# Masks of the local scores written on 64x32 tiles of TensorE in a DiT block with causal and local attention

## What is computed

```python
bk2, bv2 = (look(bk), look(bv))          # each window of 32 tokens sees itself and the window before
mask = (it < jb) | (it > jb + w) | (jb == -1)
sim = jnp.einsum('bhwie,bhwje->bhwij', bq, bk2) * QK_SCALE
sim = jnp.where(mask, -jnp.finfo(sim.dtype).max, sim)
attn = jax.nn.softmax(sim, -1)
```

## Time and profile before

| | us |
|---|---|
| median of 3 runs | 3508.06 |
| lowest, highest | 3505.7, 3515.55 |
| span of the profiled execution (first to last instruction) | 3495.1 |
| PE busy in the span | 3309.7 (95%) |
| POOL, DVE, ACT busy | 2907.1, 2951.4, 2468.4 |

### The profile page before, as it was taken

How to read it: one execution, slowest core, us unless ns; L and a number is a source line. 1 busy time by engine, 2 the same in 40 slices (tenths; PEclk the granted TensorE clock), 3 DMA queues, 4 the chain that set the end, 5 groups by cost and what they waited for, 6 DMA issues and landing times.

```text
span 3495.1 us, 158019 instructions
## 1 busy us (share of the span) xinstructions
PE 3309.7 (95%) x69988; PEld 1936.2 (55%) x69988; DVE 2951.4 (84%) x3104; ACT 2468.4 (71%) x3349; POOL 2907.1 (83%) x2483
## 2 busy tenths in 40 slices
PE   7999999779999999999999999999999999999997
PEld 4666666445555555555555555555555555555553
DVE  6888888688888988888888889888998889988873
ACT  5777777556777767777677777676877777767764
POOL 3665555588999989999899999898999999989993
PEclk9999999999999999999999999999999999999997
DMA  1000000154645545545455454555554554545452
GB/s 67 5 5 5 5 5 5 44 119 102 143 114 130 120 115 126 131 112 127 113 126 127 106 137 110 129 120 121 120 135 105 142 124 109 140 108 134 102 124 62
DMA packets 163861, 347.33 MB, mean 99 GB/s; under 512 B 32876, under 2 KB 42352, under 8 KB 153840
## 3 DMA queue, kind: packets, MB, share of 16 engines
q1 hardware_dynamic: 163184, 337.23, 40.9%
HBM read 24.62 MB, written 4.19 MB: 8 GB/s over the span
## 4 chain that ended last, share of the span: by engine, by line
PE 70%; DVE 11%; POOL 6%; issue 6%; ACT 4%; SPq 2%; DMA 1%; DVEq 0%; POOLq 0%; ACTq 0%
PE psA L697 29%; PE psB L697 23%; PE psB L559 8%; PE psA L559 6%; PE psB L754 3%; DVE h L1338 3%; DVE pt L1237 1%; SPq L490 1%; PE psA L754 1%; DVE negm L1342 1%; DVE sum L1349 1%; DVE ts L1330 1%; DVE h L1320 1%; DMA kf<-h 1%; POOL sq L1443 1%
## 5 line engine op out<-in xcount | busy, mean ns | idle before, releaser
L1410 POOL TENSOR_TENSOR pt<-wk,pt 128x256 f16<-128x256 f32 (+3 forms) x256 | 368.1, 1455 | 288.7 <-ACT pt L939 199.0
L1443 POOL TENSOR_TENSOR sq<-sq 128x512 f32<-128x512 f32 x384 | 488.5, 1281 | 79.6 <-ACT sq L1022 78.2
L1438 POOL TENSOR_TENSOR h<-h,ts 128x512 f32<-128x512 f32 x384 | 499.8, 1302 | 1.2 <-DVE ts L1330 1.2
L1439 POOL TENSOR_TENSOR h<-h,ts 128x512 f32<-128x512 f32 x384 | 497.1, 1295 | 0.0
L1338 DVE TENSOR_TENSOR h<-h,psB 128x1024 f32<-128x1024 f32 x288 | 337.8, 1215 | 57.1 <-PE psB L697 55.5
L1463 POOL TENSOR_TENSOR pb<-pb,rc 128x1024 f32<-128x1024 f32 x192 | 366.3, 1908 | 8.8 <-DVE rc L1351 8.8
L1320 DVE TENSOR_TENSOR h<-psA,t_rot 128x1024 f32<-128x1024 f32 x192 | 234.2, 1220 | 72.7 <-ACT sq L1022 65.7
L697 PE MATMUL psA<-kf,qf 64*32 64x64 f32 x18432 | 251.2, 224 | 22.0 <-issue 21.6
L697 PEld LDWEIGHTS psA<-kf,qf 64*32 64x32 f32 x18432 | 191.5, 106 | 124.8 <-issue 124.4
L1320 DVE TENSOR_TENSOR h<-psB,t_rot 128x1024 f32<-128x1024 f32 x192 | 233.4, 1216 | 26.2 <-ACT sq L1022 20.4
L1022 ACT ACTIVATE sq<-psA 128x1024 f32<-128x1024 f32 x192 | 197.0, 1027 | 63.7 <-PE psA L697 63.5
(11 more groups left out here) (368 smaller groups left out, 10242.0 us busy)
## 6 DMA issues: line engine op xcount, KB each, us to landing
qf<-h SPq DMA_DIRECT2D x768, 136.0 KB
kf<-h SPq DMA_DIRECT2D x768, 136.0 KB, 2.5
vev<-vo SPq DMA_DIRECT2D x288, 256.0 KB
vev<-vo SPq DMA_DIRECT2D x96, 192.0 KB
stage<-wqk SPq DMA_DIRECT2D x24, 256.0 KB, 5.0
stage<-wvl SPq DMA_DIRECT2D x12, 256.0 KB, 4.1
stage<-wof SPq DMA_DIRECT2D x12, 256.0 KB, 5.5
xb<-xt SPq DMA_DIRECT2D x8, 256.0 KB, 7.9
```

What stands on the lines that cost most here:

```text
L1410: e.tensor_tensor(pt[g][pr][:, :, 1, o:o + w], wk[(slot_of(s)[0] - 1) % SLOTS][:, :, 0:w], pt[g][pr][:, :, 0, o:o + w], ALU.subtract).then ...
L1438: e.tensor_tensor(halves_of(h, 0), halves_of(h, 0), t[1], ALU.subtract)
L1439: e.tensor_tensor(halves_of(h, 1), halves_of(h, 1), t[0], ALU.add).then_inc(ended["ad"])
L1443: e.tensor_tensor(sqb[c][:, 0, :], sqb[c][:, 0, :], sqb[c][:, 1, :], ALU.add).then_inc(ended["qa"])
```

## The change

The masks of a score tile are written by 16 products in place of four. Each takes 32 of the 128 columns of `lsel[rows, m, :]` as weights, and writes 32 partitions of the tile. It sits on the same 64x32 tile of the array on which the scores of these 32 partitions are computed. The moving data, and what stands in PSUM afterwards, are the same. Neither the order of the steps nor any wait is changed.

```diff
                         for m, (at, n) in enumerate(((0, 1), (64, 7))):
-                            for x in range(2):
-                                rows, at_x = slice(64 * x, 64 * x + 64), 512 * x + at
-                                mm(o[:, at_x:at_x + 64 * n].rearrange("p (a s) -> p a s", a=n), lsel[rows, m, :],
-                                   keyid[rows, :].unsqueeze(1).to_broadcast([64, n, 2 * W]), m == 0, False,
-                                   tile_position=(64 * x, 0))
+                            for to in range(0, 128, 32):
+                                for x in range(2):
+                                    rows, at_x = slice(64 * x, 64 * x + 64), 512 * x + at
+                                    mm(o[to:to + 32, at_x:at_x + 64 * n].rearrange("p (a s) -> p a s", a=n),
+                                       lsel[rows, m, to:to + 32],
+                                       keyid[rows, :].unsqueeze(1).to_broadcast([64, n, 2 * W]), m == 0, False,
+                                       tile_position=(64 * x, to))
```

## The result

| | before | after |
|---|---|---|
| median, us | 3511.81 (4 runs) | 3559.97 (4 runs) |
| lowest, highest | 3505.7, 3518.58 | 3550.86, 3566.55 |
| ratio, with its 95% interval | | 1.0135 [1.0105, 1.0164] |
| span of the profiled execution | 3495.1 | 3560.8 |

The forecast was 3524 us, 16 us more than before, in a range up to 3543. Measured are 48 us more. The sign held, the size was a third of it. The profiled execution of after took 3563.64 us as timed, 2.8 us more than its span. So only 2 to 3 us lie around the span, and not 13. The profiled execution of before, with its 3495.1, was about 8 us shorter than the shortest timed run and not a typical one (or it ran on another chip, which these runs don't tell).

The account below looks back on a forecast made before the run. TensorE (PE), busy 95% of the span, was taken as the bound. Dense-code cost 0.54 less sparse gain 0.15 gave +0.39 us per item, +17 us over 44 items, less 1: 3508 to 3524 us, range 3512 to 3540 (with rivals 3497 to 3543).

Parts of the forecast that it names:

- What bounds the kernel: Whole kernel: TensorE (PE) is the bound; its gains or losses in the local stage arrive at 75 to 80 percent.
- Part 1, the saving of 0.10 us per score tile: Masks to scores: no shape change there, 0.245 us in place of 0.32; 0.10 us saved per tile, 19 us for 192.
- Part 2, the block: TensorE's instruction supply: blocks of about 256 arrive 3.5 to 4 us after being asked for; shorter-running blocks are stretched to that.
- Part 2, dense places, 0.54 us per item: Behind pv and ss: 24 more instructions cost 0.36 us, paid in three items of four; the array saving is worth nothing.
- Part 2, sparse places, a gain of 0.15 us per item: Behind op and tp: 24 more instructions are free, the 0.10 us saving is kept, counted half behind op.
- The sum: 0.54 - 0.15 = +0.39 us per item, times 44 items as the last eight count half: +17 us, less 1 us.
- The level of the start: Whole run: median taken as 13 us above the profiled span of 3495 us, so 3508 us before the change.
- That the supply has room: Rival, chance 0.2: instruction supply has room, so the array saving arrives; 3496 us.
- both cancel: Rival, chance 0.13: dense places pay 0.36 us in two items of five, balanced by savings kept; 3509 us.
- Streams at half pace: Rival, chance 0.08: 16-bit data on eight tiles stream at half pace, each score tile 0.09 us slower; 3534 us.
- That the gap isn't from the shape: Rival, chance 0.07: gap ahead of scores comes from a new step's waits or loads; tile saves nothing, supply costs; 3532 us.
- What would show it: Signs: masks to scores 0.24 to 0.25 us, next step after 0.6, 18 more packets, stops 60 us or more, 256 instructions apart.

Follow-up runs that it names:

- e1_dense: Narrow masks only at the two dense-code score tiles per item (behind pv and ss), against before: 3550.39 us, ratio 1.0109.
- e2_sparse: Narrow masks only at the two sparse-code score tiles per item (behind op and tp), against before: 3524.43 us, ratio 1.0035.
- e6_bare_sparse: Before with the masks of the two sparse-code score tiles per item left out, part of the computation missing: 3488.41 us, ratio 0.9984.
- e4_split: Before with the 512-column products of op, f and fo cut in two, 102 more instructions per item in sparse code: 3525.77 us, ratio 1.0035.
- e9_before_again: The kernel before, unchanged, run again for a profile of a typical execution: 3512.99 us.
- e10_after_again: The changed kernel, unchanged, run again on one chip with before for a typical profile: 3561.25 us, ratio 1.014 to before.
- e3_count: Sixteen mask products per score tile on the old 64x128 tiles, eight blocks of 64 columns, against before: 3560.7 us, ratio 1.0127.
- e8_half: Masks on 64x64 tiles, 8 products per score tile, 8 instructions more than before: 3513.14 us, ratio 1.0056.
- e7_twelve: The change with 12 mask products per score tile in place of 16, same narrow tiles, against before: 3521.66 us, ratio 1.008.
- e5_bare_dense: Before with the masks of the two dense-code score tiles per item left out, part of the computation missing: 3489.75 us, ratio 0.9998.

## Why the prediction was right in kind and wrong in size

**What bounds the kernel**: right. PE's lines hold the chain, and the loss appeared in PE's stops, in no other engine's work. But the 75 to 80 percent at which TensorE's time should arrive at the end were not right for time saved: of 31 us taken from the array at the sparse places 5.6 arrived, at the dense ones 0.7.

**Part 1, the saving of 0.10 us per score tile**: its parts were right, its sum wrong. The gap of the shape change went and masks to scores fell to 0.23 us, where 0.245 was forecast. The gap ahead of the masks stayed, as said (0.15 us from the last `pv` product to the first mask, before and after). But the step behind the scores starts 0.69 us after the masks, not 0.60: 0.01 to 0.02 us are kept. The step that failed is the silent assumption that the scores keep their 7 ns from start to start. Behind narrow masks they don't: the last twelve start 3 to 47 ns apart. Whether this is the supply of instructions, for which the gap had given time, or the load of eight tiles, these runs don't settle. By the sum's own terms, 0.15 us per item fall away.

**Part 2, the block**: the reading of 256 was right, and better than its working. The prediction spread the bytes of the queue over the instructions of all engines, 57 bytes each; over TensorE's own 142527 it is 64 bytes, and 256 exactly. The records that it called missing are TensorE's semaphore instructions: by their starts, 2002.89 to 2006.70 and 2006.70 to 2011.44 hold 256 instructions each, three of them for semaphores. The shortest distance of two packets is 3.3 us, a little under the 3.5 of the prediction.

**Part 2, dense places, 0.54 us per item**: the mechanism and the rate were right, the share was not. `e1_dense` gives 38/48 = 0.8 us per item for the two places, where full payment of 0.36 at both would be 0.72. Counting three items in four took the blocks without a visible stop for blocks with room. Many have none: the block that begins at 2006.70 does so 1.46 us behind the end of its packet, as after a stop, though the array never stood still, and so do most of those that begin within 1.2 to 1.7 us of a packet's end (124 of 197 in before).

**Part 2, sparse places, a gain of 0.15 us per item**: wrong in sign, and the largest error of the sum. `e2_sparse` gives 12/48 = 0.25 us more per item. Two steps failed. The gain was not there (part 1, and `e6_bare_sparse` shows that even 0.32 us taken away at these places bring 5.6 us out of 31, not 75 to 80%). And 24 instructions more, which the prediction took as free because "nothing stops there", are not free in a block of 8.6 us. `e4_split` shows the same with other instructions, at 2.5 ns each, while here it is 5 ns. That the edges of later blocks move into dense code would explain it, but it was only argued, and why the price is twice as high here isn't settled.

**The sum**: 0.8 + 0.25 = 1.05 us per item, x 48 = 50 us, against 0.39 x 44 - 1 = 16. Of the 34 us that were missing, the sparse places make 0.40 x 48 = 19, the dense ones 0.26 x 48 = 12, and the last eight items with the 1 us taken off 3. Counting the last eight half was wrong too: from the mask group behind `tp` of item 40 to that of item 48, 461.8 us became 468.8 between `e9_before_again` and `e10_after_again`, 0.9 us per item, against 1.0 in the 39 items before.

**The level of the start**: the prediction took the 13 us between span and median for time around the span. It is 2 to 3 us. The profiled execution of before was short, and its 39.8 us of stops were 44.7 in a typical one. This moved the forecast little, since the difference was added to the median.

**The rivals.** That the supply has room, and that both cancel, are refuted by the result and by `e1_dense`. Streams at half pace are refuted by the 0.23 us. That the gap isn't from the shape is refuted too, by after, by `e3_count`, where it came back with the old shape, and by `e8_half`, where the one ahead of the masks went. That the tile then saves nothing, as that rival said, came true all the same, for another reason. The Trainium skill's figure, "TensorEngine Tiling (Array Packing)", Instruction Overhead, some 60 cycles for each matmul, would have made 0.4 us of the 16 masks: the trace disagrees, they take 0.23.

**What would show it**: the counts of matmuls and packets came as said, the stops grew to 84 us where "60 or more" was said, and they lie at every 256th instruction. The 0.6 us to the step behind the scores and the shorter sparse stretches did not come.

## What to carry to other kernels

Before a step is cut into more and smaller instructions, read how long the code around it takes per 256 instructions of the engine, semaphore instructions included. Where this is already the length at which blocks arrive (here about 3.9 us), an instruction more costs about its share, here some 15 ns, whether the array shows a stop or not. And don't count saved array time as a gain at a fixed share: look at the pace of the step behind a gap before the gap is called idle, and at what the engine would wait for next. Here 31 us less in the array brought 6 us at one pair of places and 1 at the other. Last, compare the profiled span with the timed runs before its stops are taken for typical.

## What the runs showed of the hardware that was not expected

- TensorE's instructions come in packets of 16384 bytes, 256 instructions each. No two packets start closer than 3.2 us in any of these traces, though one takes only about 1.1 us to move, and 106 of the 108 stops of after at the edges of blocks end 1.2 to 1.7 us behind the end of a packet.
- Score matmuls on 64x32 tiles start 7 ns apart behind masks of 64x128 (0.238 us for 32), and over 0.315 us behind 16 masks of 64x32. Why is open (`e7_twelve`).
- A change of tile shape between products costs about 0.1 us: 0.04 us without it and 0.15 with it, from `pv` to the masks (`e8_half`, before).
- Bf16 streams on eight 64x32 tiles side by side run at full pace: 448 columns on each within the 0.23 us.
- 31 us of array time taken out of the dense code moved the end by 0.9998 [0.9981, 1.0015] (`e5_bare_dense`). That 768 instructions less gave nothing either, while 2304 more cost 38 us, is not explained.
- The same program took 3511 us on two chips and 3491 us on a third. On the third an instruction packet took 0.99 to 1.02 us in the median, on the two others 1.11 to 1.15; whether this is the cause no run tests.
